# A two-block audio tower on one Trainium2 core: mixture bias in fp16 terms, causal attention with stationary values, finer steps, new orders, and 197 unused TensorE products in the first round

## The reference

```python
h = tok(x)                                  # 5 taps, ReLU, normalisation over the batch
h = h + softmax_attention(layernorm(h))     # 8 heads of 16, band bias near the diagonal
h = h + top2_experts(layernorm(h))          # 8 experts, hidden 256, GELU (kind 0)
h = h + linear_causal_attention(layernorm(h))   # 8 heads, values of 64, elu+1 features
# last block, on hx = layernorm(layernorm(h)) * g + b
q, k, v = hx @ Wq, hx @ Wk, hx @ Wv         # 2 heads of 64, q and k l2-normalised
attn = softmax(where(causal, q @ k.T / 8, -big)); y = (attn @ v) @ Wo
gate = softmax(y @ gate_W + gate_b)
eo = gelu(y @ W1[e] + b1[e]) @ W2[e] + b2[e]    # 8 experts, hidden 512 (kind 1)
h = h + sum_e gate[e] * eo
```

## Time and profile before

| | |
|---|---|
| time, median of 3 runs | 4183.73 us (4181.23 to 4189.27) |
| time of the profiled execution | 4183.28 us |
| its span, first to last instruction | 4181.6 us |
| mean granted TensorE clock | 0.984 |
| TensorE busy | 3994.9 us, 96% |
| VectorE, ScalarE, GpSimd busy | 78%, 66%, 61% |

### The profile page before, as it was taken

How to read it: one execution, slowest core, us unless ns; L and a number is a source line. 1 busy time by engine, 2 the same in 40 slices (tenths; PEclk the granted TensorE clock), 3 DMA queues, 4 the chain that set the end, 5 groups by cost and what they waited for, 6 DMA issues and landing times.

```text
span 4181.6 us, 104776 instructions
## 1 busy us (share of the span) xinstructions
PE 3994.9 (96%) x41344; PEld 3003.6 (72%) x41344; DVE 3258.6 (78%) x8879; ACT 2767.7 (66%) x4797; POOL 2531.2 (61%) x2494
## 2 busy tenths in 40 slices
PE   9589999999999999999999999999999999999988
PEld 4256777777777777777777777777777777777766
DVE  4367887878888777888878888878878887887866
ACT  4236776766767666677776767776676777667654
POOL 2136666666666666666666666666666666666656
PEclk9679999999999999999999999999999999999999
DMA  6100100010110000111000011100111110010100
GB/s 184 40 28 29 31 27 23 16 31 29 31 31 27 21 20 29 31 31 31 19 22 26 29 31 31 31 19 18 30 29 31 31 31 19 17 31 29 29 16 7
DMA packets 137083, 127.62 MB, mean 31 GB/s; under 512 B 28944, under 2 KB 135376, under 8 KB 136592
## 3 DMA queue, kind: packets, MB, share of 16 engines
q1 hardware_dynamic: 136592, 120.91, 9.9%
HBM read 71.05 MB, written 49.55 MB: 29 GB/s over the span
## 4 chain that ended last, share of the span: by engine, by line
PE 80%; DVE 7%; ACT 6%; issue 3%; DMA 2%; SPq 1%; POOL 1%; ACTq 0%; DVEq 0%; POOLq 0%
PE pf L1313 14%; PE pf L1315 13%; PE pf L1314 13%; PE pa L1574 8%; PE pa L1313 4%; PE pa L1315 4%; PE pa L1314 4%; PE pa L1359 3%; PE pa L1460 3%; PE pa L1556 3%; PE pa L1422 2%; PE pa L1446 2%; PE pa L1654 2%; DVE h L1297 2%; ACT hid L902 2%
## 5 line engine op out<-in xcount | busy, mean ns | idle before, releaser
L680 POOL TENSOR_TENSOR hid_lo<-hid,hid_hi 128x504 f16<-128x504 f32 x1536 | 1793.0, 1177 | 1132.3 <-DVE hid_hi L1278 1132.2
L902 ACT ACTIVATE hid<-pf,vec 128x504 f32<-128x504 f32 x1536 | 1017.2, 679 | 469.7 <-PE pf L1315 377.1
L1313 PE MATMUL pf<-w_hi,hid_hi 128*126 128x128 f16 x6144 | 1129.5, 223 | 9.4 <-DVE h L1297 6.5
L1315 PE MATMUL pf<-w_hi,hid_lo 128*126 128x128 f16 x6144 | 1115.0, 221 | 0.0
L1314 PE MATMUL pf<-w_lo,hid_hi 128*126 128x128 f16 x6144 | 1114.7, 221 | 0.0
L1313 PEld LDWEIGHTS pf<-w_hi,hid_hi 128*126 128x126 f16 x6144 | 843.2, 137 | 136.4 <-DVE h L1297 60.7
L1314 PEld LDWEIGHTS pf<-w_lo,hid_hi 128*126 128x126 f16 x6144 | 844.4, 137 | 31.1
L1315 PEld LDWEIGHTS pf<-w_hi,hid_lo 128*126 128x126 f16 x6144 | 845.8, 138 | 0.0
L1278 DVE CAST hid_hi<-hid 128x504 f16<-128x504 f32 x1536 | 774.3, 523 | 35.2 <-ACT hid L902 26.6
L1297 DVE SCALAR_TENSOR_TENSOR h<-pf,gates,h 126x128 f32<-126x128 f32 x2048 | 572.9, 341 | 112.3 <-PE pf L1315 109.4
L1313 PE MATMUL pf<-xf_hi,w_hi 128*128 128x504 f16 x1536 | 581.8, 379 | 21.6 <-ACT hid L902 20.3
(11 more groups left out here) (208 smaller groups left out, 7401.7 us busy)
## 6 DMA issues: line engine op xcount, KB each, us to landing
qk_spread<-terms SPq DMA_DIRECT2D x224, 126.0 KB, 2.5
qk_spread<-terms SPq DMA_DIRECT2D x192, 63.0 KB, 2.3
y_scratch<-hid SPq DMA_DIRECT2D x32, 252.0 KB, 2.1
y_in<-y_scratch SPq DMA_DIRECT2D x32, 252.0 KB, 3.2
terms<-qk_hi SPq DMA_DIRECT2D x32, 252.0 KB, 2.4
terms<-qk_lo SPq DMA_DIRECT2D x32, 252.0 KB, 2.4
qk_spread<-terms SPq DMA_DIRECT2D x32, 252.0 KB
terms<-ot_hi SPq DMA_DIRECT2D x32, 252.0 KB, 2.4
```

Source lines behind the costliest of these rows:

```text
L680: nc.gpsimd.tensor_tensor(hid_lo[:, c % 8], hid[:, c % HIDS], hid_hi[:, c % 8], ALU.subtract).then_inc(hid_lo_done[c % 2], 1)
L902: nc.scalar.activation(hid[:, c % HIDS], pf[:, c % 2, 0:TOK], func, bias=vec[:, bias:bias + 1]).then_inc(F["hid_ready"], 1)
L1313: nc.tensor.matmul(out, ah, bh, start=start, stop=False, skip_group_check=skip)
L1315: return nc.tensor.matmul(out, al, bh, start=False, stop=stop, skip_group_check=skip)
```

## The change

- **Bias in fp16 terms.** The gates are written as three fp16 blocks (high, high, low) and b2 as three (high, low, high). One fp16 product with an fp16 identity turns the gates, and four fp16 products per mixture, with 96 of 128 rows in use, give the bias. VectorE gets two small operations per gate (`split_gates`). b2 is loaded by 12 DMAs in place of 4, and GpSimd splits it once. TensorE no longer waits for b2 before the first transpose, but before the first bias product.
- **Causal attention with stationary values.** VectorE scales the probabilities before they are turned. The values of one head (64 columns) are then stationary and 252 or 126 query columns move. The two heads write the two halves of the partitions of one bank. The result comes out turned, and the last `turn` with its four transposes is gone.
- **Finer steps.** Many steps are cut in two, and each engine's string has only letters for steps in which that engine has something to do. `norm_stats` is split in two.
- **New orders.** All 15 strings are new.
- **Unused products.** PE_START has 197 letters `w`. Each is one fp16 product of 128x504 into bank 2 of `pf` that nobody reads. ROUND and END have none.

```diff
-            pe.wait_ge(small_loaded, 32 + 16 * TILES)
+            pe.wait_ge(small_loaded, 32)
...
-                nc.tensor.transpose(pa[a][:, GATES_T[a], 0:TILE], gates_all[0:TILE, a],
-                                    ident[0:TILE, 0:TILE]).then_inc(SS[a]["gate_turned"], 1)
+                nc.tensor.matmul(pa[a][:, GATES_T[a], 0:TILE], gate_terms[0:TILE, a], ident16[0:TILE, 0:TILE],
+                                 start=True, stop=True).then_inc(SS[a]["gate_turned"], 1)
...
+                if a == 0 and p == 0:
+                    pe.wait_ge(b2_split, 2)
                 for i in range(TILES):
-                    last = nc.tensor.matmul(pa[a][0:TILE, BIAS2[a], i * D:(i + 1) * D], gate_t[a][:], b2[:, a, i],
-                                            start=True, stop=True)
+                    last = nc.tensor.matmul(pa[a][0:TILE, BIAS2[a], i * D:(i + 1) * D], gate_t[a][:],
+                                            b2_terms[:, a, i], start=True, stop=True)
...
+            def split_gates(a, p):
+                S = SS[a]
+                dve.wait_ge(S["gate_made"], n(p + 1))
+                nc.vector.tensor_copy(gate_terms[0:TILE, a, 0:64].rearrange("p (s c) -> p s c", s=2),
+                                      gates_all[0:TILE, a].unsqueeze(1).to_broadcast([TILE, 2, TILES * EXPERTS])
+                                      ).then_inc(S["gate_hi"], 1)
+                dve.wait_ge(S["gate_hi"], n(p + 1))
+                nc.vector.tensor_tensor(gate_terms[0:TILE, a, 64:96], gates_all[0:TILE, a], gate_terms[0:TILE, a, 0:32],
+                                        ALU.subtract).then_inc(S["gate_ready"], 1)
...
+                for b in range(2):
+                    dve.wait_ge(S1["p2_ready"], n(p * 4 + 2 * b + 2))
+                    nc.vector.reciprocal(inv_sum[0:TILE, 4 * b:4 * b + 4],
+                                         row_sum[0:TILE, 2 * b:2 * b + 2].rearrange("p t h -> p (t h)")
+                                         ).then_inc(S1["rs_rec"], 1)
+                    dve.wait_ge(S1["rs_rec"], n(p * 2 + b + 1))
+                    for hd in range(HEADS2):
+                        i = 2 * b + hd
+                        for qt, c in halves:
+                            at = 4 * b + 2 * qt + hd
+                            last = nc.vector.tensor_scalar(p2[i][0:TILE, c], p2[i][0:TILE, c],
+                                                           inv_sum[0:TILE, at:at + 1], None, ALU.mult)
+                        last.then_inc(S1["p2_scaled"], 1)
+                    yield
...
+                def causal_values(b):
+                    pe.wait_ge(S1["p2t_ready"], n(p * 4 + 2 * b + 2))
+                    for kt, first, width in ((0, 0, SEQ), (1, TILE, TILE)):
+                        for hd in range(HEADS2):
                             c0 = 2 * D + hd * HEAD2
+                            last = nc.tensor.matmul(pa1[head_rows(hd), TURN, b * SEQ + first:b * SEQ + first + width],
+                                                    qkv[0:TILE, 2 * b + kt, c0:c0 + HEAD2],
+                                                    fs1[0:TILE, hd, kt * SEQ:kt * SEQ + width], start=(kt == 0),
+                                                    stop=(kt == 1), skip_group_check=True)
+                    last.then_inc(S1["turned"] if b else S1["pv2_done"], 1)
...
+            def unused():
+                evicted = 0
+                for i, part in enumerate(PE_START):
+                    if part != "w":
+                        continue
+                    experts = PE_START[:i].count("o") // CHUNKS0
+                    if experts > evicted:
+                        pe.wait_ge(F["gated"], n(experts))
+                        evicted = experts
+                    nc.tensor.matmul(pf[:, 2, 0:TOK], W("up1", 0, 128)[0], W("up1", 0, TOK)[0], start=True, stop=True)
+                    yield
```

546 lines of the change are left out of this document (245 added, 301 removed).

## The result

The changed kernel takes 4113.6 us (median of four runs, 4109.5 to 4117.0). The kernel before took 4183.35 beside it. The ratio is 0.9831 (95% interval 0.9814 to 0.9848): 70 us faster, where 167 were forecast, and 29 us above the upper end of the range. The sign was right, the size was not.

A forecast was written before the change was run, and what follows sets the result against it. TensorE, busy 96%, was taken to set the steady round of 122.36 us. Rounds -129, START -33 and END -5 summed to -167 us, from 4183.7 to 4017 us; range 3960 to 4085, the forecast's own 3990 to 4050.

The forecast's parts named there:

- -2.9 us a round: Steady rounds: TensorE's work falls by this much, from causal attention (-1.45) and fp16 bias with gates' turns (-1.4).
- 0.05 to 0.1 for the change of form: Causal value products: allowance in us for changing form, within 0.75 us a sequence.
- -1.4 a round: Steady rounds: TensorE's waits shrink, 2.3 us of the present 4 gone and 0.9 new, bounds 0 and -3.
- the two repeated waits on ScalarE: TensorE's waits at the second turn of probabilities and first causal scores get cover; some 1.9 us a round.
- Rival 4: Rounds: slower, VectorE falls behind and TensorE waits at each expert's end; 4247 us at 0.35 us each, chance 0.05.
- What is taken from that work comes off the round as long as no wait grows.: Steady rounds: TensorE's work sets the 122.36 us round, so cutting that work shortens it.
- 23 net: START: unused products raise the clock, saving 27 us, less 4 for real work they delay.
- the 10 of the finer steps and b2: START: finer steps and less work in two pairs -8 us, first transpose no longer behind b2 -2.0.
- Forecast -5: END: one pair's 2.9 us of work and 2 for waits come off, bounds 0 to -10.
- rival 1: Whole kernel: the work goes, the waits stay; rounds 87, START 20, END 3 us off, 4073 us, chance 0.22.

The follow-up runs named there:

- Experiment 7: Changed kernel with the scaling of a head's probabilities cut to one operation of 8 columns on VectorE: 4103.2 us, ratio 0.9787.
- Experiment 17: Changed kernel with GpSimd's squares cut from 1024 to 64 columns, nothing moved: 4078.9 us, ratio 0.9732.
- experiment 1: Kernel before with the fp16 bias alone, including the split of gates and b2, in the old orders: 4177.4 us, ratio 0.9984.
- experiment 5: Kernel before with each mixture's bias product made for one of its four tiles only: 4220.2 us, ratio 1.0068.
- (10): Changed kernel with bias products and gates' turn in fp32 again, the split of the gates still made but unused: 4169.1 us, ratio 0.9954.
- experiment 4: Changed kernel without its 197 unused products in START: 4124.7 us, ratio 0.9854.
- experiment 9: Changed kernel with 52 unused products more, in END where TensorE waits: 4110.0 us, ratio 0.981.
- experiment 8: Changed kernel with TensorE's two turns of the gates one h later and the first bias one o later in ROUND: 4158.7 us, ratio 0.992.
- 12: Changed kernel with the additions that make v moved behind the softmax of the second gates on VectorE: 4129.2 us, ratio 0.9855.
- experiment 2: Kernel before with the causal attention's stationary values alone, in the old orders: 4390.8 us, ratio 1.0487.
- experiment 11: Kernel before with three of a mixture's four bias products cut from 128 columns to 8: 4185.5 us, ratio 0.9988.

## Why the prediction was wrong

**The work.** "-2.9 us a round" was nearly right for the instructions named: value products -0.85 and transposes -0.43 make -1.28 (forecast -1.45), bias and turns -1.31 (forecast -1.4), in sum -2.6. What I left out is what the new order does to the rest: 0.95 us a round of small gaps, some 0.6 of it at the changes of form. My 0.05 to 0.1 for the change of form was charged to the new products alone. It was not counted over the order, and it leaves out the late second product behind a change. The net is -1.64.

**The waits, the step that failed.** "-1.4 a round" was the largest error: measured -0.12. I had seen correctly that the two repeated waits on ScalarE would get cover; they are gone. For the new ones I took 0.9 us; the three on VectorE alone came to (80.7 - 6.5) / 31 = 2.4 us a round. I judged them by VectorE's load, which I had right to 0.6 us, and called that load hidden. Experiment 7 shows that 1.6 us of load are worth 0.27. Experiment 17 shows what is not hidden: where a VectorE copy starts beside a GpSimd operation, it lasts as long as that one, and the first adds of an expert queue behind it. With that one hold gone, the stalls fall from 4.30 to 3.17 us a round, 1.13 of the 1.28 that the forecast had missed. Rival 4 named the place, the wait at the end of an expert, with the wrong mechanism (the queue behind the new scalings) and the wrong sign in sum: that wait grew from 6.5 to 38.3 us, not to over 100.

**"What is taken from that work comes off the round as long as no wait grows."** The sentence holds, but in the old orders its condition does not. In the old orders 1.4 us less work, with the four VectorE operations that come with it, made the waits grow by 1.1 (experiment 1), and 1.3 us less made the round longer (5). In the new orders the same bias counts in full (10). Busy 96% does not tell which of the two one has.

**The two parts are not separable from the orders.** I treated the orders as the thing that carries the edits. They are worth 256 us against the same edits in the old ones, and there the causal part is a loss of 200, in which the clock and the instruction blocks may have a part.

**START.** The first transpose started at 132.56 in place of 134.44: -1.9, forecast -2.0. The clock rose as forecast, but the products were worth 12 us and not 23 net. By the share of TensorE on the chain, 23 net of 127 slow us were to come back, 18%; experiment 4 says 12 of 87, 14%. Nor did all slow time go: some 18 us are left. The rest, -13, is a little more than the 10 of the finer steps and b2.

**END.** Forecast -5, measured +11.5. I looked for the clock only where it was low before. In the new END it falls for 34 us; experiment 9 gives the 10 us back.

**The chances.** The measured mixture is nearest to rival 1 (the work goes, the waits stay, 4073 us), with END (+15) and the small gaps (+0.95 x 31 = 29 us) on top: 4117. Neither was among the bounds, and so the range ended too low. That the sum comes so near to 4113.6 is partly luck: START gave 5 us more than in rival 1, and the named work 0.3 us a round less.

**What stays open.** Why moving one step costs 1.6 us a round in experiment 8 and 0.5 in 12 is not settled by the waits listed. How the loss of experiment 2 divides between order, clock and instruction blocks is open too. The DMA wait of 10.6 us was not taken away by itself. The price of the changes of form, and of the late second product behind them, was read from the trace and not tested by an order with fewer of them.

## What to carry to other kernels

Before a term "waits go" is written down, run a version that frees the engine's time and changes nothing else: it tells what that time is worth, and here 1.4 us were worth 0.7 in one order and 1.9 in another. See in its trace that it freed what it was meant to free, and that no instruction block moved beside a transfer. Where VectorE and GpSimd both work, read the longest duration of each VectorE operation beside its median. A longest of five times the median, as here, tells that a GpSimd operation held it, whatever the busy shares. Whether TensorE waits behind that place decides if it costs anything, and moving the operation can move the hold. And look at the clock in every part of the new program, not only in the parts where it was low.

## What the runs showed of the hardware

- A VectorE copy of fp32 to fp16 in SBUF (0.42 us) takes up to 2.16 us when it starts beside a GpSimd operation, and a product of 32 columns 0.92 or 1.39 in place of 0.19. The adds that read PSUM (0.34 us) showed nothing of the kind, 0.35 at most.
- One 16 KB block of instructions beside a 252 KB store delays its landing: 2.2 to 2.7 us without, 3.3 to 4.2 with one in the kernel before, 3.7 to 4.5 in experiment 5. There are 328 such blocks, and 325 with 12 TensorE instructions a pair fewer. Which transfer it meets depends on the number of instructions in a round, so a kernel can get slower when instructions are taken away.
- A change of the array's form costs TensorE 0.09 us, in and out. Behind the way back the second product starts 0.05 us late, in 19 places a round of the changed kernel; with products of 504 columns (8 places in the kernel before) it is 0.01.
- An fp32 matmul instruction of 8 columns held TensorE 0.11 us, as one of 128 columns did (experiment 11).
- The clock fell in END of the changed kernel behind 6.8 us in which TensorE was busy 3.8, and stayed at half through 17 us in which it was busy all the time. With 52 unused products in the waits of END it was at 1.00.
- Half-clock time has no fixed price: 87 us in START cost 12, and in END 34 us cost 10, 24 us cost 6 and 21 us cost 4.
